# Moving the third unit's gate run and weight split from behind the attention phase into its last steps

## The reference

```python
x = _layernorm(x + attn(x))
x = _layernorm(x + ffn(x))

# attn: 16 heads of 32, rmsnorm on q and k, rope, a window of 256 keys, softmax, Wo
# ffn:
logits = x @ W_router.T
rw, sel = jax.lax.top_k(softmax(logits), 2)               # 8 experts, 2 per token
sh = _silu_and_mul(x @ Ws_gate_up, 1408) @ Ws_down         # shared expert
shared_out = sh * jax.nn.sigmoid(x @ W_sgate.T)
gu = jnp.einsum('th,ehi->eti', x, We_gate_up)
h = _silu_and_mul(gu, 352)
eo = jnp.einsum('eti,eih->eth', h, We_down)
sparse_out = jnp.einsum('eth,te->th', eo, combine)
return shared_out + sparse_out
```

## Time and profile before

| | |
|---|---|
| median of three runs | 1036.63 us |
| lowest, highest | 1036.13, 1036.85 us |
| the profiled execution | 1036.27 us |
| its span, first to last instruction | 1034.4 us |
| mean granted TensorE clock | 0.996 of full speed |
| busy: TensorE | 1013.3 us, 98% |
| busy: VectorE | 774.6 us, 75% |
| busy: ScalarE | 638.3 us, 62% |
| busy: GpSimd | 449.6 us, 43% |

### The profile page before, as it was taken

How to read it: one execution, slowest core, us unless ns; L and a number is a source line. 1 busy time by engine, 2 the same in 40 slices (tenths; PEclk the granted TensorE clock), 3 DMA queues, 4 the chain that set the end, 5 groups by cost and what they waited for, 6 DMA issues and landing times.

```text
span 1034.4 us, 19741 instructions
## 1 busy us (share of the span) xinstructions
PE 1013.3 (98%) x7088; PEld 839.6 (81%) x7088; DVE 774.6 (75%) x1165; ACT 638.3 (62%) x1311; POOL 449.6 (43%) x537
## 2 busy tenths in 40 slices
PE   6999999999999999999999999999999999999996
PEld 4677777777777777788888888888888888888885
DVE  6878888888888886596766777677677777667466
ACT  4666666666666765333766666666666666766444
POOL 2688888788888851000122222222222222221174
PEclk9999999999999999999999999999999999999998
DMA  5101111111111025635899999999999999999564
GB/s 195 55 24 43 33 34 33 41 48 33 34 44 33 22 84 167 223 88 171 251 269 257 269 274 261 266 267 256 257 280 264 262 264 278 253 252 252 121 215 155
DMA packets 120981, 171.36 MB, mean 166 GB/s; under 512 B 10114, under 2 KB 63746, under 8 KB 120804
## 3 DMA queue, kind: packets, MB, share of 16 engines
q1 hardware_dynamic: 111856, 149.54, 45.4%
q0 software_dynamic: 8736, 20.45, 11.9%
q10 hardware_dynamic: 292, 0.10, 0.0%
HBM read 151.45 MB, written 23.07 MB: 169 GB/s over the span
## 4 chain that ended last, share of the span: by engine, by line
PE 94%; DVE 1%; POOL 1%; issue 0%; DVEq 0%; POOLq 0%
PE probT_ps L615 6%; PE proj_ps L584 5%; PE proj_ps L582 5%; PE proj_ps L583 5%; PE oT_ps L631 5%; PE score_ps L603 4%; PE gate_ps L1658 4%; PE gate_ps L1660 4%; PE gate_ps L1659 4%; PE up_ps L1658 4%; PE up_ps L1660 4%; PE up_ps L1659 4%; PE down_ps L1693 4%; PE down_ps L1695 4%; PE down_ps L1694 4%; PE e_up_ps L1735 3%
## 5 line engine op out<-in xcount | busy, mean ns | idle before, releaser
L1053 POOL DMA_INDIRECT sum_dram<-rows,target_i x39 | 67.7, 1737 | 356.6 <-ACT rows L1170 356.6
L1482 DVE TENSOR_TENSOR e_lo<-e_raw,e_hi 128x1408 fp32r<-128x1408 f32 x78 | 126.8, 1625 | 49.0 <-ACT e_hi L1144 48.9
L1144 ACT CAST e_hi<-e_raw 128x1408 fp32r<-128x1408 f32 x78 | 107.5, 1378 | 52.3 <-PE e_up_ps L1745 51.7
L340 ACT ACTIVATE prob<-score_ps,nbias 128x256 f32<-128x256 f32 (+1 forms) x256 | 118.1, 471 | 5.3 <-DVE nbias L469 5.3
L272 POOL TENSOR_TENSOR probT<-probT,masks 128x256 f32<-128x256 f32 x128 | 91.7, 744 | 49.3 <-DVE probT L499 49.2
L1487 DVE TENSOR_TENSOR ed_lo<-ed_raw,ed_hi 128x1024 fp32r<-128x1024 f32 x39 | 47.8, 1226 | 60.5 <-ACT ed_hi L1152 43.6
L469 DVE TENSOR_REDUCE nbias<-score_ps 128x2 f32<-128x512 f32 (+1 forms) x128 | 86.3, 674 | 4.4
L1059 POOL DMA_INDIRECT rows<-x_dram,token_i x39 | 49.3, 1265 | 88.8 <-DVE target_i L1437 65.1
L347 ACT COPY probT<-probT_ps 128x512 f32<-128x512 f32 x64 | 37.6, 587 | 79.5 <-PE probT_ps L615 79.4
L582 PE MATMUL proj_ps<-wqkv_lo,xT_hi 128*128 128x512 f32 x180 | 78.0, 433 | 1.2 <-ACT squares L361 1.2
L1658 PE MATMUL gate_ps<-x_hi,gu_lo 128*128 128x512 f32 x180 | 72.1, 401 | 0.6 <-DVE gu_lo L1325 0.6
(11 more groups left out here) (286 smaller groups left out, 2984.0 us busy)
## 6 DMA issues: line engine op xcount, KB each, us to landing
e_raw<-in_We_gu SPq DMA_DIRECT2D x78, 704.0 KB
ed_raw<-in_We_down SPq DMA_DIRECT2D x39, 512.0 KB, 5.3
raw_ring<-in_Ws_gu SPq DMA_DIRECT2D x58, 256.0 KB
wd_raw<-in_Ws_down SPq DMA_DIRECT2D x44, 256.0 KB
gu_raw<-in_Ws_gu SPq DMA_DIRECT2D x30, 256.0 KB
ed_raw<-in_We_down SPq DMA_DIRECT2D x39, 192.0 KB, 6.7
xT_in<-in_xT SPq DMA_DIRECT2D x16, 256.0 KB, 2.8
x_in<-in_x SPq DMA_DIRECT2D x16, 256.0 KB, 3.1
```

Source lines behind the costliest of these rows:

```text
L340: nc.scalar.activation(prob[:, g % 2, h, seen], score_ps[:, h, seen], ACT.Exp, bias=nbias[:, s % 2, head:head + 1], scale=1.0, accum_out=r ...
L1144: nc.scalar.copy(e_hi[:, half * HK:(half + 1) * HK, :, 0:I_MOE], raw_parts(i, half)).then_inc(e_hi_made, 1)
L1482: nc.vector.tensor_tensor(e_lo[:, part, :, 0:I_MOE], raw_parts(i, half), e_hi[:, part, :, 0:I_MOE].bitcast(FP32), ALU.subtract).then_inc(e ...
```

## The change

The split of the third unit's gate and up weights (`split_gu(2)`, unit n = 2) is moved on ScalarE from step 16, group 2 to the end of step 15, group 1, and on VectorE from step 16, group 2 to the end of step 15, group 2. The run `gate(2)` is moved on TensorE from the end of step 17, group 0 to the hook `between` of step 16, group 0: behind the last group's probability transposes and ahead of the turn of x. Nothing is added or taken away, and the semaphores and their values stay.

```diff
--- before.py
+++ after.py
@@ -1222,6 +1222,7 @@
                     split_gu(1)
                 if at == NB - 1 and g == 1:
                     take_up()
+                    split_gu(2)
                 if at == NB - 1 and g == 2:
                     take_gate(1)
                 if at == NB - 1 and g == 3:
@@ -1233,7 +1234,6 @@
                 if at == NB and g == 1:
                     silu_of(1)
                 if at == NB and g == 2:
-                    split_gu(2)
                     split_hidden(1)
                 if at == NB and g == 3:
                     split_gu(3)
@@ -1518,9 +1518,10 @@
                     split_wd(1)
                     multiply(0)
                     split_hidden(0)
+                if at == NB - 1 and g == 2:
+                    split_gu(2)
                 if at == NB and g == 2:
                     multiply(1)
-                    split_gu(2)
                     split_hidden(1)
                 if at == NB + 1 and g == 0:
                     split_gu(3)
@@ -1764,6 +1765,8 @@
                     gate(1)
                 if (at, g) == (LAST, 3):
                     pe.wait_ge(gate_taken, 2)
+                if (at, g) == (LAST + 1, 0):
+                    gate(2)
                 if (at, g) == (LAST + 1, 1):
                     up(1)
 
@@ -1772,7 +1775,6 @@
                 if (at, g) == (LAST + 1, 1):
                     down(0)
                 if (at, g) == (LAST + 2, 0):
-                    gate(2)
                     router_parts(0)
                     up(2)
                     router_parts(1)
```

## The result

| | before | changed |
|---|---|---|
| median of 12 runs each | 1036.13 us | 1038.88 us |
| lowest, highest | 1035.2, 1037.49 | 1036.84, 1041.16 |
| ratio, with its 95% interval | | 1.0025 [1.0017, 1.0032] |
| the profiled execution, its span | 1036.27, 1034.4 | 1039.88, 1038.0 |

The changed kernel is 2.75 us slower by the medians. The time, 1038.88, lies in the stated range of 1036.2 to 1039.2, but the forecast was 1.4 us of loss, about half of what came. The spread of the single runs has grown from 2.3 to 4.3 us, which the prediction didn't foresee.

What follows compares the result with a forecast made beforehand. TensorE was taken as the bound, busy 1013.3 of 1034.4 us. A new wait before the second router run, net +1.4 us, on the 1036.63 us median gave 1038.0 us, range 1036.2 to 1039.2.

Steps and rivals of the forecast that it cites:

- Part 1: Step 16, group 0: gate(2) starts at once at 390.63 us, and the turn of x comes 2.24 us later.
- Part 2: Step 15: the moved split fits idle time of ScalarE and VectorE and costs nothing, within 0 and 0.5 us.
- the named cover: Step 15: the probT copy waits anyway for transposes until 380.95 us, hiding a 0.4 to 0.5 us slip of ScalarE's oT cast.
- Part 3: Step 17: without gate(2) the first router run waits for the last residual addition; only 0.15 us of gain is left.
- Part 4: Chain from turn of x through x1, store, weights and VectorE's copy shifts 2.18 us; second router run waits 1.50, +1.4 us.
- the 1.35 us of the sum: Second router run at 411.04 us, 1.35 us later than the 409.69 of before.
- the 0.9 us to spare: Before the change, VectorE's copy was done 0.89 us ahead of the second router run (408.80 against 409.69).
- (a): Fourth unit's weights land 1.5 us or more earlier than the shift, so no second-router wait: 1036.5 us; chance 0.11.
- (b): The clock falls after the one 1.5 us wait, costing 1.70 us more: 1039.7 us; chance 0.08.
- (c): Weights or a load behind them land later still, each us adding one: 1038.7 us and above; chance 0.07.
- (d): Neither the addition nor the copy is waited for, and the whole 0.7 us gain stays: 1035.9 us; chance 0.02.
- the row of before: Trace of the kernel before: 5.34 us from weights' issue (399.50) to ScalarE's cast (404.84), preferred over the 3.7 us estimate.

Runs made afterwards that it cites:

- e9: The changed kernel unaltered, timed and profiled again against the kernel before: 1038.58 against 1036.21 us, ratio 1.0023.
- e1: The changed kernel with gate(2) back in step 17, only the split moved; against the kernel before: 1036.76 against 1036.51 us, ratio 1.0005.
- e4: The changed kernel with gate(2) behind the turn of x in the same group; against the kernel before: 1037.33 against 1036.51 us, ratio 1.0010.
- e2: The changed kernel without SyncE's wait for the store of block 14's x1; against the kernel before: 1036.95 against 1036.51 us, ratio 1.0005.
- e7: The kernel before with block 14's x1 stored a second time and waited for, nothing moved: 1037.90 against 1036.54 us, ratio 1.0013.
- e3: The changed kernel with fourth unit's weights and third down weights loaded ahead of the x1 store; against the kernel before: 1036.83 against 1036.51 us, ratio 1.0002.
- e5: The changed kernel with VectorE's late weight splits behind its copy of the first router part; against the kernel before: 1037.09 against 1036.54 us, ratio 1.0006.
- e11: The changed kernel unaltered, fourth profile, one run: 1036.87 us; its store landed in 2.02 us.
- e8: The changed kernel with e3's loads, fourth-unit splits later on both engines, three up(2) matmuls before the first router run; against before: 1035.84 against 1036.54 us, ratio 0.9995.

## Why the prediction was right, and where it was not

**The range, met by luck.** The range was laid around a median of 1036.63 us for the kernel before. The twelve runs beside the changed kernel have 1036.13. As a difference the range was from 0.4 below to 2.6 above, and the measured 2.75 lies just outside; in e9 it was 2.37. So the mechanism below is what was right, and the time inside the range owes 0.5 us to the lower median.

**Part 1, right.** gate(2) started 0.85 us behind the transposes, without a wait. The turn moved by 2.25 us, forecast 2.24.

**Part 2, right.** The splits in step 15 cost nothing: e1 has the distances of before to 0.01 us. ScalarE's cast of oT came 0.35 us late (380.88 instead of 380.00 and the 0.53), and the copy behind it by 0.01 (381.53 instead of 380.99 and the 0.53), as the named cover said.

**Part 3, right.** The residual sum became a wait, 0.44 us by the trace. The first router run was 0.06 us sooner than before, forecast 0.15. The missing 0.09 is the release: the sum took 0.06 from a turn, and a router run started 0.14 us behind the end of the addition (405.38 + 0.69 to 406.21).

**Part 4, right in its mechanism, and short by half in its size.** Every link that it named was met in its place, and five experiments cut or lengthened the chain at four points: the turn (e4), the wait for the store (e2, and e7 from the other side), the loads (e3), the order of VectorE (e5). The step that failed is "every link is released by the one before it, so all shift by 2.18". It took the store's 2.02 us over as a constant. That holds in one of four profiles, and there the loss is the 1.35 us of the sum. That it meets the sum to the hundredth is luck: the copy came 2.09 us later and not 2.18, and the router run started 0.15 us behind it and not 0.06. In three profiles the store took 1.4 to 1.6 us more, and with the 0.9 us to spare used up already, the run came 1.3 to 1.8 us behind that of e11. The sum also left out GpSimd's `rstd`, which bounds the copy once the weights are early (e3, e4). The median of +2.75 us lies between the two kinds, with e9's fall of the clock on top in some executions; how often each comes I can't say from four profiles.

**The rivals.** (a), the transfer in time, did not occur. (b), the fall of the clock, was given 0.08 as a case of its own, with a price of 1.70 us. It came in one profile of four, for 1.58 us, behind a wait of 2.7 us; behind e11's wait of 1.34 the clock stayed at 1.00. (c), the later landing, had 0.07, and is what three profiles show. The mistake in the chances was to weigh the landing as one fixed number with some noise, though the sum had just made it the link that everything hangs on. The spread from 1036.84 to 1041.16 fits this: in the profiles the loss is 1.35 without either, 2.7 to 3.1 with a late store, and 4.3 with a slow clock behind it. The three slowest of the 24 executions of the changed kernel (1041.16, 1040.96 and e9's profiled 1040.51) are those with the lowest mean granted clock, 0.993, 0.992 and 0.992, where the others have 0.994 to 0.998. But 1040.33 and 1040.18 have 0.995 and 0.996, and no profile says what they lost. (d) did not occur.

**The transfer's time and the rule on the clock.** From the weights' issue to the cast the row of before had 5.34 us, the changed kernel 409.22 - 403.76 = 5.46 and its other three profiles 5.01 to 5.22. The row decided, and was right to. The Trainium skill (DMA: Bandwidth & Descriptors, the part on two cost components) gave an estimate of 3.7 us for it, and no profile agrees. The fit of the Trainium skill was measured, per transfer, on those that GpSimd issues, while these are issued by SyncE. On the clock, e9 had 0.62 and 0.52 behind a wait of 2.74 us, while waits of 3.10 and 2.63 us in two other profiles left it at 1.00. The Trainium skill (TensorE: Matmul & The Clock Gate, the part on the gate) has it drop after idleness; e9 agrees, and the other two don't show it.

## What to carry to other kernels

Where TensorE is full, a small piece of work put into a wait should be as long as the wait: 0.59 us held three matmuls (0.56 us gained in the trace, with intervals of the times that just reach no change), and the nine others only delayed a 128x512 turn on which a chain over four engines hung. Before work is moved ahead of an instruction, follow that instruction's result to the end of its chain, through stores, loads and the small instructions of other engines too, and count how much each in-order queue has to spare at the last link. If a chain that was slack becomes the bound, its transfers' bad cases count in full, not their typical ones.

## What the runs showed of the hardware that I had not expected

- A store of 256 KB was seen by the waiting queue 2.01 to 2.04 us after its issue in ten profiles, and after 3.40 to 3.64 us in three. In these three, and in no other, one packet of the instruction queue ran about 0.5 us behind the issue, and the last packets of the store came singly over 1.3 to 1.5 us. What causes it stays open.
- After an idle of 2.74 us the granted clock fell to 0.52 to 0.62 for 4 us once, and after 3.10 and 2.63 us, in the same place of the same program, it didn't.
- Three large matmuls put between a turn and a router run took 0.86 us, where three in the middle of a run take 0.69 (e8).
- GpSimd's two one-column instructions for `rstd` took 0.19 and 0.55 us in the eleven profiles in which VectorE stood idle beside them, 1.07 and 0.88 us in e3 and e4 and 0.19 and 1.50 us in e2, in which VectorE ran a split of weights at the same time.
